# Products in bursts of two key tiles, one 128-column transpose for the row maxima, stacks loaded three groups ahead

## The chip, the cores and the metric

The kernel runs on one core of one Trainium2 chip. The time is that of one execution on the device in microseconds, given as the median of several runs. A core has five engines that run side by side, each with its own list of instructions: TensorE (PE; PEld are its weight loads), VectorE (DVE), ScalarE (ACT), GpSimd (POOL) and SyncE (SP), which here only issues DMA transfers. They wait for each other on semaphores: an instruction waits until a counter has reached a value, and everything behind it on the same engine waits with it.

## What is computed

Four blocks run one after the other on 4 batches of 512 tokens of width 256: a cross attention with a mask (xa0), a self attention (sa0) and a mixture of eight experts (me0), a second cross attention (xa1) and a second mixture (me1). The change touches the three attentions. Each has 16 heads of width 16:

```python
q = split_heads(query @ Wq.T + bq)
k = split_heads(key @ Wk.T + bk)
v = split_heads(value @ Wv.T + bv)
scores = jnp.einsum('bhqd,bhkd->bhqk', q, k) / np.sqrt(HEAD_DIM).astype(np.float32)
attn = jax.nn.softmax(scores, axis=-1)
ctx = jnp.einsum('bhqk,bhkd->bhqd', attn, v)
```

In xa0 the scores are masked before the softmax. Everything is in 32-bit floats; the output of a block is added to its input.

## The kernel before

**Stages.** An attention has a projection stage and an attending stage. The projection goes through the four batches. It makes q and k, splits each value into three 16-bit parts, and stores the parts in DRAM (`q_parts`, `k_parts`, line L700, SP). The attending stage goes through 16 groups, four per batch (`g` is the group in its batch, `G` its number in the stage). A group is four heads of one batch. Its stacks, `qst[g]` and `kst[g]`, are loaded back from DRAM (`load_stacks`, L334): 96 rows, six products of parts times 16 head columns, for each head and token. There is one pair of stack buffers for each of the four `g`.

**Units.** A group has 16 units, `u` = 0 to 15. A unit is one tile of 128 x 512 scores for one head. It is made twice:

- by `scores` (L958), query rows on the partitions, for the row maxima. VectorE reduces each tile to its maximum (`maximum`: L373 with the mask, L377 without). This side runs ahead by 28 units (`LEAD`), so at unit `u` of group g it works on group g + 1 or g + 2.
- by `transposed_scores` (L971), key rows on the partitions, with three further rows that carry minus the row maximum in three 16-bit parts (99 rows). In xa0 a second matmul (L975) adds the mask. ScalarE takes the exponential of each tile (L885) into `probs`.

Both sides rotate over three PSUM banks (`DEEP` = 3), so a tile can be made when the one three units earlier has been read. At a border between batches the rotation starts anew (`before`): the first tile of a batch waits for the last one of the batch before.

**Row maxima.** When the 16 maxima tiles of a group are reduced, `split` on VectorE (L1125 to L1131) writes the three parts into `mparts`. At `u` = 8 TensorE transposes them (`maxima`, L993, four transposes of 12 columns, one for each tile of 128 queries), ScalarE copies the result into `mT`, 12 rows of 512 (L898), and SP moves it into rows 96 to 98 of the next group's `qst` (`shift`, L792). The next group's first `transposed_scores` waits for that.

**Products.** `products` (L985) multiplies the exponentials with the values: for one tile of 128 keys, four matmuls, one for each head, each in its own 32 columns of the array, so the four run side by side. In 32-bit floats each is two instructions in the trace, so a burst is eight. The four key tiles of a group come after units 5, 9 and 13 and, the last one, after unit 1 of the next group. ScalarE then copies the sums (L891), TensorE turns them at `u` = 12 (`turn`, L1016), and VectorE divides by the row sums after unit 13 (`normalise`, L1139 to L1144). In later batches TensorE also turns the output of the batch before (`turn_out`, L1025, in g 1) and projects it (`project_out`, L1036, in g 2 and 3), and VectorE adds it after unit 5 of g 2 and 3 (`residual`, L1165 in xa1, L1171 in sa0, there with `block_input`, L1153 and L1157).

**Order.** Nothing is scheduled by a program: each engine's list is written out by hand in the loops over `g` and `u`. SP's is, for each group: wait until the group two before has been used up and load the stacks of g + 2, wait for `mT` and issue the shift of g + 1, then a piece of the weights of a later stage. The first two groups' stacks are loaded inside the projection stage, between the stores of the second and the third batch.

Of the kernel before, what the change touches and what calls it, by code (L numbers as in the profile page):

```python
# [35 lines left out]
P = 128  # L36
# [4 lines left out]
HG = 4  # L41
# [30 lines left out]
class Memory:  # L72


    def __init__(self, nc, ctx):
# [24 lines left out]
        self.mres = sb("mres", [P, T, HG])  # L100
        self.mparts = sb("mparts", [P, T, PARTS, HG], BF16)
        self.mT = sb("mT", [PARTS * HG, S], BF16)
        self.den = sb("den", [P, T, HG])
# [116 lines left out]
class Attention:  # L220


    def __init__(self, nc, stage, mem, dram, name, w, cross, norms, affine, cols, rows, masked, self_block,
# [40 lines left out]
        self.stacks = [sig(f"stacks{s}", 32) for s in range(NG)]  # L264
        self.shift = [sig(f"shift{s}", 16) for s in range(NG)]
        self.s_ps = sig("s_ps", UNITS)
# [411 lines left out]
def project_sync(sp, a):  # L678
# [34 lines left out]
    def rest_of_batches():  # L713
        context(1)
        if a.fresh:
            sp.wait_ge(a.setup, 13)
            for s in range(NG):
                sp.dma_start(mem.kst[s][ROWS:KROWS, :, :].rearrange("r h (i n) -> r (h i) n", n=P),
                             mem.ones[0:PARTS, :].unsqueeze(1).to_broadcast([PARTS, HG * S // P, P]))\
                  .then_inc(a.shift_ones.sem, 16)  # L720
        if a.masked:
            load_mask(sp, a, 0)
        for b in range(0, B - 2):
            body(b, b + 2)
        for n in range(QK):
            sp.wait_ge(a.stored[n].sem, a.stored[n].at(1))
        load_stacks(sp, a, 0, 0)
        load_stacks(sp, a, 0, 1)
        body(B - 2, None)
        body(B - 1, None)  # L730
# [24 lines left out]
LAST_TURN, LAST_OUT = (5, 2), (3, 4)  # L755
LATE = 2

M_STEP, TURN_STEP = 8, 12
# [25 lines left out]
def attend_sync(sp, a, meanwhile, then=None):  # L784
# [3 lines left out]
    def shift(b, g):  # L788

        G = NG * b + g  # L790
        sp.wait_ge(a.m_sb.sem, a.m_sb.at(G, 1))
        sp.dma_start(mem.qst[g][ROWS:KROWS, :, :], mem.mT[:, :]).then_inc(a.shift[g].sem, 16)  # L792

    def body(b, first, last):
        for g in range(NG):
            G = NG * b + g
            ahead = (b, g + 2) if g < 2 else (b + 1, g - 2)
            if not (last and g >= 2):
                if first and g == 2:
                    for n in range(QK):  # L800
                        sp.wait_ge(a.stored[n].sem, a.stored[n].at(B))
                if not (first and g < 2):
                    sp.wait_ge(a.st_ps.sem, a.st_ps.at(G - 1))
                load_stacks(sp, a, *ahead)
# [71 lines left out]
def attend_scalar(act, a, meanwhile):  # L876
# [16 lines left out]
    def maxima(G, used=None):  # L893
        act.wait_ge(a.m_ps.sem, a.m_ps.at(G, 1))
        if used is not None:
            b, g = used
            act.wait_ge(a.shift[g].sem, a.shift[g].at(b, 16))
        act.activation(mem.mT[:, :], ps[0:PARTS * HG, MISC, 0:S // 2].bitcast(BF16), ACT.Copy)\  # L898
           .then_inc(a.m_sb.sem, 1)
# [43 lines left out]
def attend_tensor(pe, a, meanwhile):  # L943
# [17 lines left out]
    def transposed_scores(b, g, u, first):  # L961
# [4 lines left out]
        if u == 0:  # L966
            pe.wait_ge(a.shift[g].sem, a.shift[g].at(b, 16))
            if a.masked and g == 0:
# [9 lines left out]

    def products(G, g, kt):
        pe.wait_ge(a.p_exp.sem, a.p_exp.at(G, HG * (kt + 1)))  # L980
        if kt == 0:
            pe.wait_ge(a.vg_ready.sem, a.vg_ready.at(G, 1))
            pe.wait_ge(a.ot_sb.sem, a.ot_sb.at(G))
        for h in range(HG):
            ins = pe.matmul(ps[h * VW:(h + 1) * VW, OB, :], mem.vg[g % 2][:, kt, h, :], mem.probs[:, kt, h, :],  # L985
                            start=(kt == 0), stop=(kt == T - 1))
        ins.then_inc(a.pv.sem, 1)

    def maxima(G):
        pe.wait_ge(a.cut.sem, a.cut.at(G, CUTS))  # L990
        take_misc()
        for t in range(T):
            ins = pe.transpose(ps[0:PARTS * HG, MISC, t * P // 2:(t + 1) * P // 2].bitcast(BF16),  # L993
                               mem.mparts[:, t, :, :].rearrange("p a h -> p (a h)"), mem.identb[:, :])
        ins.then_inc(a.m_ps.sem, 1)
        misc[0] = (a.m_sb.sem, a.m_sb.at(G, 1))
# [45 lines left out]
    def body(b, first, last):  # L1042
# [4 lines left out]
        for g in range(NG):  # L1047
            G = NG * b + g
            for u in range(UNITS):
# [8 lines left out]

                at = u - HG - LATE + 1
                if at < 0 and u == LATE - 1 and not (first and g == 0):  # L1060
                    products(G - 1, (g - 1) % NG, T - 1)
                if at >= 0 and at % HG == 0:
                    products(G, g, at // HG)
                if g == 1 and not first and u in OUT_TURNS:
# [37 lines left out]
    G = B * NG - 1  # L1102
    products(G, NG - 1, T - 1)
    turn(G)
# [8 lines left out]
def attend_vector(dve, a, meanwhile, beside=None):  # L1113
# [4 lines left out]
    def split(G):  # L1118
# [4 lines left out]
        m = mem.m[:, :, :]  # L1123
        hi, mid, lo = (mem.mparts[:, :, i, :] for i in range(PARTS))
        dve.tensor_scalar(hi, m, -1.0, None, ALU.mult).then_inc(a.cut.sem, 1)  # L1125
# [709 lines left out]
def program(nc, x, ctxT, mask, wa, wb, wc, cols, rows, b1c, b2, gate0, w1, w2, gate1, we, be, out):  # L1835
# [10 lines left out]
    with ExitStack() as ctx:  # L1846
# [26 lines left out]
        def constants(pool):  # L1873
# [3 lines left out]
            pool.memset(mem.ones[:, :], 1.0).then_inc(setup, 1)  # L1877
            pool.memset(mem.tri[:, :], 1.0).then_inc(setup, 1)
            pool.memset(mem.onehot[:, NT, :], 0.0).then_inc(setup, 1)
            pool.iota(mem.count_i[:, :], [[1, P]], base=0, channel_multiplier=0).then_inc(setup, 1)  # L1880
            pool.iota(mem.number_i[:, :], [[1, 1]], base=0, channel_multiplier=1).then_inc(setup, 1)
            pool.wait_ge(setup, 8)
            for eye in (mem.ident, mem.identb):
# [48 lines left out]
        with nc.Block() as block:  # L1932
# [83 lines left out]
            def _(pe):  # L2016
                pe.wait_ge(setup, 13)
                begin, rest = project_tensor(pe, xa0)
# [72 lines left out]
```

## Time and profile before

| | us |
|---|---|
| median of 3 runs | 1280.65 |
| lowest and highest | 1279.75, 1281.99 |
| the profiled execution | 1274.43 |
| its span, from first to last instruction | 1272.7 |

| engine | busy, us | share |
|---|---|---|
| TensorE matmuls | 1131.4 | 89% |
| VectorE | 838.6 | 66% |
| ScalarE | 660.4 | 52% |
| GpSimd | 210.9 | 17% |

The profiled execution is one more run beside the three. Busy time is the time in which an engine has an instruction in work; matmuls overlap in TensorE's pipeline, so what one costs is read from the distance between starts, not from its duration. The attending stages lie at about 63 to 300 us (xa0), 407 to 630 us (sa0) and 937 to 1162 us (xa1). In the timelines a row is one instruction or several alike behind each other (xN), with start and length; in brackets stands how long the engine was idle before it and what it then waited for.

### The profile page before, as it was taken

How to read it: one execution, taken by the hardware profiler on the slowest of the kernel's cores; microseconds unless marked ns; L12 is line 12 of the kernel's file. 1: busy time of each engine (PE TensorE's matmuls, PEld its weight loads, DVE VectorE, ACT ScalarE, POOL GpSimd, SP SyncE). 2: the span in 40 equal slices, each digit the busy share in tenths (PEclk: the TensorE clock that was granted, in tenths of full speed). 3: DMA queues.
4: the chain of work that ended last, by engine and by line, in shares of the span. 5: the costliest groups of instructions: out<-in, count | busy, mean ns of one | idle time of the engine just before them, and what ended most of it. 6: DMA issues, size and time to landing. Idle time of an engine off the chain costs nothing. (4 is left out here: it accounts for less than half of the span.)

```text
span 1272.7 us, 17810 instructions
## 1 busy us (share of the span) xinstructions
PE 1131.4 (89%) x5693; PEld 544.0 (43%) x5722; DVE 838.6 (66%) x2112; ACT 660.4 (52%) x1341; POOL 210.9 (17%) x272
## 2 busy tenths in 40 slices
PE   7889999999997999999967999996989999998390
PEld 4423343434453223343364666664523333335370
DVE  5878777777478888888762222223888888876722
ACT  3346666666533677677722333332537767674250
POOL 4310000000143000000202222211520010102154
PEclk9989999999999899999967999998989999999795
DMA  8953321221048433543291140103873323211064
GB/s 265 309 169 93 79 57 28 81 52 26 2 154 291 103 91 90 132 97 93 72 375 33 31 161 28 27 13 102 263 241 91 90 59 89 60 37 57 25 171 144
DMA packets 100706, 139.40 MB, mean 110 GB/s; under 512 B 8452, under 2 KB 82632, under 8 KB 99208
## 3 DMA queue, kind: packets, MB, share of 16 engines
q1 hardware_dynamic: 96536, 128.03, 33.6%
q0 software_dynamic: 4080, 10.23, 2.9%
q8 instruction: 48, 0.79, 0.3%
q14 instruction: 42, 0.34, 0.1%
HBM read 86.30 MB, written 52.17 MB: 109 GB/s over the span
## 5 line engine op out<-in xcount | busy, mean ns | idle before, releaser
L885 ACT ACTIVATE r<-ps 128x512 f32<-128x512 f32 x768 | 427.4, 600 | 211.9 <-PE ps L971 122.1
L377 DVE TENSOR_REDUCE m<-ps 128x1 f32<-128x512 f32 x512 | 320.9, 682 | 45.2 <-PE ps L958 44.9
L971 PE MATMUL ps<-r 99*128 99x512 bf16 x768 | 294.3, 388 | 5.6 <-ACT r L885 5.6
L958 PE MATMUL ps<-r 96*128 96x512 bf16 x720 | 280.9, 393 | 20.5 <-DVE m L377 7.0
L373 DVE CUSTOM_DVE_ANT_0 r<-ps,r 128x512 bf16<-128x512 f32 x256 | 170.2, 690 | 60.2 <-PE ps L958 59.6
L985 PE MATMUL ps<-r 128*32 128x512 f32 x1536 | 204.9, 605 | 4.9 <-ACT r L885 3.3
L971 PEld LDWEIGHTS ps<-r 99*128 99x128 bf16 x768 | 74.4, 98 | 211.7 <-ACT r L885 157.3
L958 PEld LDWEIGHTS ps<-r 96*128 96x128 bf16 x720 | 71.3, 99 | 105.9 <-DVE m L377 24.3
L861 POOL COPY r<-r 128x256 f32<-128x256 f32 x48 | 19.0, 399 | 542.1 <-PE ps L985 542.1
L1660 DVE COPY r<-ps 128x512 f32<-128x512 f32 x46 | 31.8, 691 | 91.9 <-PE ps L1707 91.9
L1707 PE MATMUL ps<-r 128*128 x184 | 87.8, 621 | 2.7 <-issue 0.4
L1619 ACT ACTIVATE r<-ps,cols 128x128 f32<-128x128 f32 x46 | 18.5, 453 | 137.8 <-PE ps L1698 137.8
L657 PE MATMUL ps<-r,w 128*128 128x512 f32 x192 | 88.2, 596 | 0.5 <-issue 0.5
L975 PE MATMUL ps<-r,identb 128*128 128x512 bf16 x227 | 87.5, 386 | 0.0
L1732 PE MATMUL ps<-r 128*128 x368 | 83.3, 380 | 1.1 <-ACT r L1629 1.1
L1671 DVE TENSOR_TENSOR r<-ps,r 128x256 f32<-128x256 f32 x46 | 19.5, 425 | 97.0 <-PE ps L1732 68.8
L1732 PEld LDWEIGHTS ps<-r 128*128 128x128 f32 x368 | 69.9, 190 | 20.1 <-issue 11.9
L589 ACT ACTIVATE r<-ps,cols 128x512 bf16<-128x512 f32 x48 | 32.9, 686 | 86.9 <-PE ps L657 72.7
L985 PEld LDWEIGHTS ps<-r 128*32 128x32 f32 x1536 | 30.3, 108 | 84.0 <-ACT r L885 65.3
L537 POOL TENSOR_TENSOR r<-r 128x512 bf16<-128x512 f32 x48 | 55.0, 1164 | 65.5 <-ACT r L594 65.5
L644 PE MATMUL ps<-w,r 128*128 128x256 f32 x192 | 45.5, 392 | 13.6 <-DMA w<-in_wa 7.4
L1629 ACT ACTIVATE r<-ps,b1c 128x128 f32<-128x128 f32 x184 | 49.9, 382 | 12.9 <-PE ps L1715 12.8
(151 smaller groups left out, 1220.5 us busy)
## 6 DMA issues: line engine op xcount, KB each, us to landing
r<-q_parts SPq DMA_DIRECT2D x48, 384.0 KB, 5.2
r<-k_parts SPq DMA_DIRECT2D x48, 384.0 KB, 6.0
k_parts<-r SPq DMA_DIRECT2D x24, 384.0 KB, 3.3
q_parts<-r SPq DMA_DIRECT2D x24, 384.0 KB, 3.1
r<-in_w SPq DMA_DIRECT2D x16, 512.0 KB, 4.9
r<-in_w SPq DMA_DIRECT2D x8, 1024.0 KB, 14.4
k_parts<-r SPq DMA_DIRECT2D x24, 256.0 KB, 3.3
q_parts<-r SPq DMA_DIRECT2D x24, 256.0 KB, 3.1
```

The costliest lines, as they stand in the source:

```text
L373: ins = dve.tensor_tensor_reduce(mem.junk[bank], mem.ps[:, bank, :], mem.mbS[:, t, :], 1.0, FLOOR, ALU.add, ALU.max, out)
L377: ins = dve.tensor_reduce(out, mem.ps[:, bank, :], AX.X, ALU.max)
L537: pool.tensor_tensor(mem.parts[n][:, 2, :], mem.res[n % 2], mem.parts[n][:, 1, :], ALU.subtract).then_inc(a.lo.sem, 1)
L657: ins = pe.matmul(ps[:, QK_BANK + n, :], a.w[:, 0 if of_query(n) else 1, c, (n % C) * P:(n % C + 1) * P], src[:, c, :], start=(c == 0), st ...
L885: act.activation(mem.probs[:, u // HG, u % HG, :], ps[:, ST + (UNITS * g + u) % DEEP, :], ACT.Exp, scale=SCALE).then_inc(a.p_exp.sem, 1)
L958: pe.matmul(ps[:, led_bank(n), :], mem.qst[g][0:ROWS, h, t * P:(t + 1) * P], mem.kst[g][0:ROWS, h, :], start=True, stop=True).then_inc(a.s ...
L971: ins = pe.matmul(out, mem.kst[g][0:KROWS, h, kt * P:(kt + 1) * P], mem.qst[g][0:KROWS, h, :], start=True, stop=not a.masked)
L975: ins = pe.matmul(out, mem.identb[:, :], mem.mbT[:, batch, kt, :].rearrange("p b n -> p (b n)"), start=False, stop=True)
L985: ins = pe.matmul(ps[h * VW:(h + 1) * VW, OB, :], mem.vg[g % 2][:, kt, h, :], mem.probs[:, kt, h, :], start=(kt == 0), stop=(kt == T - 1))
L1629: ins = act.activation(mem.midT[:, f, :], ps[:, TM[f // 4], (f % 4) * P:(f % 4 + 1) * P], ACT.Relu, bias=mem.b1c[:, bass.ds(e * FT + f, 1)])
L1707: ins = pe.matmul(ps[:, UP[k], :], mem.xT[j % 2][:, c, :], w, start=(c == 0), stop=(c == C - 1))
L1732: ins = pe.matmul(ps[:, DOWN[j % 2], 0:D], mem.midT[:, f, :], w, start=(f == 0), stop=(f == FT - 1))
```

## The change

Three things are altered.

1. **Products.** `TOGETHER` = 2: two key tiles are multiplied in one burst of 16 instructions. The first burst comes after unit 9, the second after unit 1 of the next group. Each waits for the exponentials of both its tiles.
2. **Row maxima.** `mparts` becomes one tile of 128 x 128 (48 columns used, the rest zero, set once by GpSimd), and one transpose of 128 columns takes the place of the four. `mT` has 48 rows of 128. The shift becomes four transfers of 3 x 4 x 128 in place of one of 3 x 4 x 512.
3. **Stacks.** `AHEAD` = 3: a group's stacks are loaded when the group three before starts, as soon as the group that used the same buffers has been used up. Three pairs are loaded inside the projection stage.

```diff
--- before.py
+++ after.py
@@ -98,8 +98,8 @@
         self.mres = sb("mres", [P, T, HG])
-        self.mparts = sb("mparts", [P, T, PARTS, HG], BF16)
-        self.mT = sb("mT", [PARTS * HG, S], BF16)
+        self.mparts = sb("mparts", [P, P], BF16)
+        self.mT = sb("mT", [PARTS * T * HG, P], BF16)
         self.den = sb("den", [P, T, HG])
@@ -262,7 +262,7 @@
         self.stacks = [sig(f"stacks{s}", 32) for s in range(NG)]
-        self.shift = [sig(f"shift{s}", 16) for s in range(NG)]
+        self.shift = [sig(f"shift{s}", 16 * T) for s in range(NG)]
         self.s_ps = sig("s_ps", UNITS)
@@ -724,8 +724,8 @@
             sp.wait_ge(a.stored[n].sem, a.stored[n].at(1))
-        load_stacks(sp, a, 0, 0)
-        load_stacks(sp, a, 0, 1)
+        for g in range(AHEAD):
+            load_stacks(sp, a, 0, g)
         body(B - 2, None)
@@ -754,6 +754,8 @@
 LATE = 2
+AHEAD = 3
+TOGETHER = 2
 
@@ -789,18 +791,20 @@
         sp.wait_ge(a.m_sb.sem, a.m_sb.at(G, 1))
-        sp.dma_start(mem.qst[g][ROWS:KROWS, :, :], mem.mT[:, :]).then_inc(a.shift[g].sem, 16)
+        for t in range(T):
+            sp.dma_start(mem.qst[g][ROWS:KROWS, :, t * P:(t + 1) * P],
+                         mem.mT[t * PARTS * HG:(t + 1) * PARTS * HG, :]).then_inc(a.shift[g].sem, 16)
 
     def body(b, first, last):
         for g in range(NG):
             G = NG * b + g
-            ahead = (b, g + 2) if g < 2 else (b + 1, g - 2)
-            if not (last and g >= 2):
-                if first and g == 2:
+            ahead = (b, g + AHEAD) if g + AHEAD < NG else (b + 1, g + AHEAD - NG)
+            if not (last and g + AHEAD >= NG):
+                if first and g + AHEAD == NG:
                     for n in range(QK):
                         sp.wait_ge(a.stored[n].sem, a.stored[n].at(B))
-                if not (first and g < 2):
-                    sp.wait_ge(a.st_ps.sem, a.st_ps.at(G - 1))
+                if G + AHEAD >= NG:
+                    sp.wait_ge(a.st_ps.sem, a.st_ps.at(G + AHEAD - NG + 1))
                 load_stacks(sp, a, *ahead)
@@ -894,8 +898,8 @@
             b, g = used
-            act.wait_ge(a.shift[g].sem, a.shift[g].at(b, 16))
-        act.activation(mem.mT[:, :], ps[0:PARTS * HG, MISC, 0:S // 2].bitcast(BF16), ACT.Copy)\
+            act.wait_ge(a.shift[g].sem, a.shift[g].at(b, 16 * T))
+        act.activation(mem.mT[:, :], ps[0:PARTS * T * HG, MISC, 0:P // 2].bitcast(BF16), ACT.Copy)\
            .then_inc(a.m_sb.sem, 1)
@@ -964,7 +968,7 @@
         if u == 0:
-            pe.wait_ge(a.shift[g].sem, a.shift[g].at(b, 16))
+            pe.wait_ge(a.shift[g].sem, a.shift[g].at(b, 16 * T))
             if a.masked and g == 0:
@@ -976,23 +980,21 @@
 
-    def products(G, g, kt):
-        pe.wait_ge(a.p_exp.sem, a.p_exp.at(G, HG * (kt + 1)))
-        if kt == 0:
+    def products(G, g, first):
+        pe.wait_ge(a.p_exp.sem, a.p_exp.at(G, HG * (first + TOGETHER)))
+        if first == 0:
             pe.wait_ge(a.vg_ready.sem, a.vg_ready.at(G, 1))
             pe.wait_ge(a.ot_sb.sem, a.ot_sb.at(G))
-        for h in range(HG):
-            ins = pe.matmul(ps[h * VW:(h + 1) * VW, OB, :], mem.vg[g % 2][:, kt, h, :], mem.probs[:, kt, h, :],
-                            start=(kt == 0), stop=(kt == T - 1))
-        ins.then_inc(a.pv.sem, 1)
+        for kt in range(first, first + TOGETHER):
+            for h in range(HG):
+                ins = pe.matmul(ps[h * VW:(h + 1) * VW, OB, :], mem.vg[g % 2][:, kt, h, :], mem.probs[:, kt, h, :],
+                                start=(kt == 0), stop=(kt == T - 1))
+            ins.then_inc(a.pv.sem, 1)
 
     def maxima(G):
         pe.wait_ge(a.cut.sem, a.cut.at(G, CUTS))
         take_misc()
-        for t in range(T):
-            ins = pe.transpose(ps[0:PARTS * HG, MISC, t * P // 2:(t + 1) * P // 2].bitcast(BF16),
-                               mem.mparts[:, t, :, :].rearrange("p a h -> p (a h)"), mem.identb[:, :])
-        ins.then_inc(a.m_ps.sem, 1)
+        pe.transpose(ps[:, MISC, 0:P // 2].bitcast(BF16), mem.mparts[:, :], mem.identb[:, :]).then_inc(a.m_ps.sem, 1)
         misc[0] = (a.m_sb.sem, a.m_sb.at(G, 1))
@@ -1056,11 +1058,11 @@
 
-                at = u - HG - LATE + 1
-                if at < 0 and u == LATE - 1 and not (first and g == 0):
-                    products(G - 1, (g - 1) % NG, T - 1)
-                if at >= 0 and at % HG == 0:
-                    products(G, g, at // HG)
+                at = u + 1 - LATE
+                if at == 0 and not (first and g == 0):
+                    products(G - 1, (g - 1) % NG, T - TOGETHER)
+                if at > 0 and at % (TOGETHER * HG) == 0:
+                    products(G, g, at // HG - TOGETHER)
                 if g == 1 and not first and u in OUT_TURNS:
@@ -1100,7 +1102,7 @@
     G = B * NG - 1
-    products(G, NG - 1, T - 1)
+    products(G, NG - 1, T - TOGETHER)
     turn(G)
@@ -1121,7 +1123,8 @@
         m = mem.m[:, :, :]
-        hi, mid, lo = (mem.mparts[:, :, i, :] for i in range(PARTS))
+        mparts = mem.mparts[:, 0:T * PARTS * HG].rearrange("p (t a h) -> p t a h", t=T, a=PARTS)
+        hi, mid, lo = (mparts[:, :, i, :] for i in range(PARTS))
         dve.tensor_scalar(hi, m, -1.0, None, ALU.mult).then_inc(a.cut.sem, 1)
@@ -1876,10 +1879,11 @@
             pool.memset(mem.tri[:, :], 1.0).then_inc(setup, 1)
+            pool.memset(mem.mparts[:, :], 0.0).then_inc(setup, 1)
             pool.memset(mem.onehot[:, NT, :], 0.0).then_inc(setup, 1)
             pool.iota(mem.count_i[:, :], [[1, P]], base=0, channel_multiplier=0).then_inc(setup, 1)
             pool.iota(mem.number_i[:, :], [[1, 1]], base=0, channel_multiplier=1).then_inc(setup, 1)
-            pool.wait_ge(setup, 8)
+            pool.wait_ge(setup, 9)
             for eye in (mem.ident, mem.identb):
```

In two more places a count of the setup semaphore goes from 13 to 14.

TensorE in a group of sa0 before, from the transposes at `u` = 8: L971 and L958 are the two matmuls of a unit, L985 the products.

```order
L993 MATMUL ps<-identb,mparts 12x128 x4
L971 MATMUL ps<-r 128x512
L958 MATMUL ps<-r 128x512
L985 MATMUL ps<-r 32x512 x4
L971 MATMUL ps<-r 128x512
L958 MATMUL ps<-r 128x512
```

The same place in the changed kernel: the lines are now L997, L975, L962 and L990.

```order
L997 MATMUL ps<-identb,mparts 128x128
L975 MATMUL ps<-r 128x512
L962 MATMUL ps<-r 128x512
L990 MATMUL ps<-r 32x512 x8
L975 MATMUL ps<-r 128x512
L962 MATMUL ps<-r 128x512
```

The four transposes have become one, and the second key tile's products stand directly behind the first's. The next place for products before, after unit 13, with the turn of the sums (L1016) ahead:

```order
L1016 MATMUL ps<-ident,r 128x128 x4
L971 MATMUL ps<-r 128x512
L958 MATMUL ps<-r 128x512
L985 MATMUL ps<-r 32x512 x4
```

And in the changed kernel:

```order
L1018 MATMUL ps<-ident,r 128x128 x4
L975 MATMUL ps<-r 128x512
L962 MATMUL ps<-r 128x512
L975 MATMUL ps<-r 128x512
```

Nothing stands between the units from there to unit 1 of the next group.

SP in xa0's projection stage before, where the first stacks (L334) stand between the stores of the second batch and those of the third (L700):

```order
L700 DMA q_parts<-r 128x512
L334 DMA r<-q_parts 96x4x512
L334 DMA r<-k_parts 96x4x512
L334 DMA r<-q_parts 96x4x512
L334 DMA r<-k_parts 96x4x512
L700 DMA k_parts<-r 128x3x512
```

In the changed kernel:

```order
L334 DMA r<-q_parts 96x4x512
L334 DMA r<-k_parts 96x4x512
L334 DMA r<-q_parts 96x4x512
L334 DMA r<-k_parts 96x4x512
L334 DMA r<-q_parts 96x4x512
L334 DMA r<-k_parts 96x4x512
L700 DMA k_parts<-r 128x3x512
```

The third pair has moved ahead of the stores of the last two batches.

## Rows read from the trace of the kernel before

**Rows 1.** Busy time by stretch: us, then each engine's, clock, DMA, GB/s.

```profile
200.00:300.00 100.00, 98.44 (x561) 38.67 (x569) 74.16 (x234) 63.50 (x111) 2.40 (x6) 1.00 0.23 59
...
400.00:500.00 100.00, 92.53 (x480) 29.76 (x479) 87.95 (x169) 64.06 (x122) 7.65 (x12) 0.93 0.46 120
...
1000.00:1100.00 100.00, 99.14 (x576) 37.37 (x580) 85.86 (x175) 71.53 (x137) 6.54 (x10) 1.00 0.27 70
```

**Rows 2.** Timeline of TensorE, a group of xa1: start, length, what [idle before].

```profile
1087.87 0.38 PE L958 MATMUL ps<-r 96*128 96x512 bf16 x1
1088.18 0.39 PE L993 MATMUL ps<-identb,mparts 128*12 128x128 bf16 x4
1088.50 0.39 PE L971 MATMUL ps<-r 99*128 99x512 bf16 x1
1088.72 0.38 PE L958 MATMUL ps<-r 96*128 96x512 bf16 x1
1089.04 1.06 PE L985 MATMUL ps<-r 128*32 128x512 f32 x8
1090.03 0.39 PE L971 MATMUL ps<-r 99*128 99x512 bf16 x1
```

**Rows 3.** Timeline of VectorE in xa1.

```profile
1065.94 0.16 DVE L1139 TENSOR_SCALAR den<-ps 128x16 f32<-128x16 f32 x1
...
1066.82 2.48 DVE L377 TENSOR_REDUCE m<-ps 128x1 f32<-128x512 f32 x4
1069.67 1.29 DVE L377 TENSOR_REDUCE m<-ps 128x1 f32<-128x512 f32 x2 [0.36 <-PE ps L958]
...
1071.71 1.28 DVE L377 TENSOR_REDUCE m<-ps 128x1 f32<-128x512 f32 x2
...
1086.48 0.68 DVE L1165 TENSOR_TENSOR x<-ps,x 128x512 f32<-128x512 f32 x1
```

**Rows 4.** Timelines of VectorE and TensorE in sa0, behind a residual.

```profile
517.26 0.73 DVE L1153 TENSOR_SCALAR w<-x,mv_in,rstd_in 128x256 f32<-128x256 f32 x2
...
519.36 2.47 DVE L377 TENSOR_REDUCE m<-ps 128x1 f32<-128x512 f32 x4
...
520.13 0.38 PE L958 MATMUL ps<-r 96*128 96x512 bf16 x1
...
521.66 0.38 PE L958 MATMUL ps<-r 96*128 96x512 bf16 x1
...
522.08 2.48 DVE L377 TENSOR_REDUCE m<-ps 128x1 f32<-128x512 f32 x4 [0.26 <-PE ps L958]
```

**Rows 5.** Timeline of ScalarE: first and fifteenth copy L898, sa0 and xa1.

```profile
425.79 0.57 ACT L898 ACTIVATE mT<-ps 12x512 bf16<-12x512 bf16 x1
...
616.28 0.57 ACT L898 ACTIVATE mT<-ps 12x512 bf16<-12x512 bf16 x1
...
955.95 0.57 ACT L898 ACTIVATE mT<-ps 12x512 bf16<-12x512 bf16 x1
...
1142.67 0.57 ACT L898 ACTIVATE mT<-ps 12x512 bf16<-12x512 bf16 x1
```

**Rows 6.** Timeline of VectorE in xa0: one batch's mask for the maxima.

```profile
50.42 1.80 DVE L389 TENSOR_SCALAR r<-r 128x512 bf16<-128x512 int32 x4
```

**Rows 7.** Timeline of TensorE in xa0: the first wait for a stack.

```profile
97.53 0.39 PE L958 MATMUL ps<-r 96*128 96x512 bf16 x1 [0.77 <-DMA r<-k_parts]
```

**Rows 8.** DMA issues from 38 to 56 us: size, median us to landing.

```profile
r<-q_parts SPq DMA_DIRECT2D x2, 384.0 KB, 6.8
```

**Rows 9.** Timeline of ScalarE in xa0's projection stage.

```profile
53.37 0.69 ACT L589 ACTIVATE r<-ps,cols 128x512 bf16<-128x512 f32 x1 [4.83 <-DMA k_parts<-r]
```

**Rows 10.** Timeline of SP in xa1: one issue of the shift.

```profile
956.54 0.74 SPq L792 DMA_DIRECT2D r<-mT  x1
```

**Rows 11.** DMA issues of the whole span: a small load, us to landing.

```profile
b1c<-in_b1c SPq DMA_DIRECT2D x1, 32.0 KB, 1.8
```

**Rows 12.** Timeline of ScalarE in xa1's last group.

```profile
1155.18 2.07 ACT L885 ACTIVATE r<-ps 128x512 f32<-128x512 f32 x4 [0.50 <-PE ps L971]
```

More of the change, by code:

```diff
@@ L715, in rest_of_batches @@
         if a.fresh:
-            sp.wait_ge(a.setup, 13)
+            sp.wait_ge(a.setup, 14)
             for s in range(NG):
@@ L2016, in _ @@
             def _(pe):
-                pe.wait_ge(setup, 13)
+                pe.wait_ge(setup, 14)
                 begin, rest = project_tensor(pe, xa0)
```

## The prediction

> **What bounds the kernel now.** I read the busy time by stretches first. In the masked attention (xa0) TensorE is busy 98% of a stretch and VectorE 74%; in the last attention (xa1) it is 99% and 86%, both at the full 2.4 GHz [rows 1]. Then the timelines of one group. An unmasked unit is two 512-column matmuls, L971 for the exponentials and L958 for the maxima. Such matmuls start 0.22 us apart [rows 2], so a unit takes TensorE 0.44; a masked unit has L975 as a third, 0.66. Sixteen units, four bursts of products and the transposes fill TensorE's time: TensorE sets the pace of a group. VectorE has little to spare in the unmasked stages: in xa1 it idles 0.36 us behind a burst before the next tile of scores arrives [rows 3]. Between the two engines lie three banks of scores, and that is what the change has to be tested against.
>
> **What a group costs VectorE.** Maxima come 0.60 apart (four take 2.48, one alone 0.68). The split (L1125 to L1131) stretches one of these steps to 1.44, so it adds 0.84; the quotient (L1139 to L1144) adds 0.88, from 1065.94 to 1066.82 [rows 3]. That is 16 x 0.603 + 0.84 + 0.88 = 11.37 us per group. In groups 2 and 3 of a later batch a residual comes on top: 0.68 less the overlap, 0.63, in xa1, and in sa0 with the block input 2.0 (from 517.26 to 519.36, less the overlap) [rows 3, 4].
>
> **The transpose.** From L958 to the four L993 it is 0.31, and these take 0.32 to the next L971 [rows 2]: 0.63, where L958 alone would take 0.22. So they cost 0.41. One 128-column transpose in the shape of its neighbours is a quarter of 0.22, 0.06, with no change of shape. The bounds are 0.06 and, if the change of shape still costs its 0.09 on either side, 0.24. I take 0.06, for L958 and L971 differ in rows and still follow each other at 0.22. Gain: 0.35 of TensorE's time per group. The copy of it by ScalarE gets a quarter of the columns; ScalarE waits for TensorE anyway, so nothing.
>
> **The products.** From L958 to L985 it is 0.31, that is 0.09 more than L958 needs, and from L985 to the next L971 it is 0.99 [rows 2]. The eight instructions are two passes of four at a time. One instruction lasts 0.60 and the burst 1.06, so the second pass starts 0.46 behind the first, and the last takes 0.53 with its drain. Two key tiles are four passes: 3 x 0.46 + 0.53 = 1.91 in place of 0.99 + 0.99 + 0.09. Gain: 0.16 per merged pair, two pairs per group. The bounds are 1.71, if four passes ran at the 0.43 that 512 columns at half rate take (twice 0.22) and all of the drain were hidden, and 1.98, if nothing is saved. No row shows two key tiles back to back; I take 1.91, built from the one burst that there is.
>
> The Trainium skill, "TensorE: Matmul & The Clock Gate", section "The mechanism", says that a weight load overlaps matmuls in flight only when its row group differs. All these products use the same rows; by that rule every pass would wait for the end of the one before, 4 x 0.60 or more, and the sum would grow by some 45 us. The trace speaks against it: eight such matmuls of 0.60 are through in 0.99.
>
> **What the longer burst does to VectorE** decides the sum. While TensorE is in a burst it makes no scores, and VectorE lives on the three banks. A tile of scores reaches VectorE 0.42 after its L958 starts (521.66, then 522.08). Sa0 shows the case of full banks, just behind a residual: L958 of the tenth unit starts at 520.13, as soon as the maximum begun at 519.36 is done; a burst follows; VectorE, with four maxima in hand from 519.36, is dry at 521.8, and its next begins at 522.08, idle 0.26 [rows 4]. That is the least idle that a burst of 0.99 can leave. With 1.91 it is 0.26 + 0.92 = 1.18, and a group lasts at least 11.37 + 2 x 1.18 = **13.7** us, halves of some 6.85. TensorE would need only 16 x 0.44 + 2 x 2.00 + 0.06 + 0.44 = 11.5; its turns of the output lie in its own waits now. VectorE becomes the bound in the unmasked stages, and the 0.35 + 0.32 saved on TensorE are worth nothing there.
>
> **The sum of the unmasked stages.** Between the copies L898 of the first and of the fifteenth group lie 14 intervals: 186.7 us in xa1, 190.5 in sa0 [rows 5]. After: 12.8 for the first (no quotient in it), 12 x 13.72, 13.6 for the last (VectorE has maxima for a quarter of it only); three borders between batches, where the rotation of the banks makes TensorE wait for VectorE's very last maximum, +1.04 each; four residuals, 2.5 in all or 8.0. That is 196.7 and 202.2: **+10.0** and **+11.7**. The first group's early burst goes away, worth 0.5 in each: **-1**.
>
> **The masked stage.** A unit takes TensorE 0.66 against VectorE's 0.60, half a group 1.91 + 0.09 + 8 x 0.66 + 0.06 = 7.3 against VectorE's 7.0, so TensorE stays the bound and keeps the gain: 16 x 0.35 and 31 merged pairs x 0.16, -10.6. In the first batch VectorE makes the mask of the next one between maxima, four pieces in 1.80 [rows 6], three of them inside one half: 8.4 instead of 7.3, +1.1. The stall for the stack below is 0.77. Together **-10**.
>
> **Stacks three ahead.** Seven times the first L958 of a group waited for its stack, 0.77 us the first and longest time [rows 7], 3.2 in all. These go; six lie in the unmasked intervals and are counted there. But at a stage's start the third pair of loads now stands ahead of the stores of the last two batches. There the queue is full: a load of 384 KB takes 6.8 us to land, and ScalarE waited 4.83 for the stores of k_parts, with VectorE behind it [rows 8, 9]. Another 768 KB at some 300 GB/s are 2.5 us, and two issues about 1. I take 2.0 in xa0, 1.5 in xa1 and 0.5 in sa0, where ScalarE did not wait for these stores: **+4** (0 to 7).
>
> **The shift in four pieces.** One issue takes 0.74 on SP [rows 10], some 0.78 with its gap, so the fourth starts 2.3 later. Behind the transpose come copy and hand-over (0.9), these 2.3 and a landing; small loads land in 1.8 [rows 11]: 5.0. TensorE asks for the shift 5.5 behind the transpose in an unmasked group, 7 in a masked one, and VectorE's pace gives 0.9 more. Nothing, then; with a landing of 4 it would be +1 per unmasked group. The skill's "DMA: Bandwidth & Descriptors", section "Specifications", wants at least 512 B in a piece; these have 256 B where they had 1 KB. No row here has that form, and the sum takes nothing from it.
>
> **The ends of the stages.** There ScalarE is the bound and idles 0.5 per burst [rows 12]; a double burst makes 1.4 of twice 0.5, +0.4, three times less what the output's turns hid. The last burst has two tiles behind the last exponential, +0.92. Together 1.8, three stages: **+5.4**. POOL's one more memset is done before the first weights have landed.
>
> **The sum:** 10.0 + 11.7 - 1 - 10 + 4 + 5.4 = +20 on the profiled 1274.4, so 1294.4. That run stands 6.2 below the median of 1280.65. The forecast for the median is 1280.65 + 20, **1300**.
>
> **Rivals.** A: TensorE stays the bound, since VectorE catches up in the longer stretch between bursts. For it speaks the 99% of xa1, against it the 0.26 of sa0. It would give 48 x 0.67 = -32, -3 for the stacks and +4: 1249. It decides at the length of the burst: at 1.71 an unmasked group takes 13.3, today's mean of 186.7 / 14, and the gain of xa0 decides. Chance 0.10, the faster side.
> B: the passes close up to 1.71. 87 double bursts x 0.20 = -17 against my sum, 1283. For it: 512 columns need no more. Against: the 0.46 seen. Chance 0.08, a quarter faster, half the same.
> C: the four pieces land late, and TensorE waits at each group's first L971: 30 x 1, some 1330. Chance 0.07.
> D: TensorE, now with gaps, is granted 1.2 GHz for stretches, as between 400 and 500 us, where the mean is 0.93 and TensorE busy less [rows 1]. 1320 or more. Chance 0.03.
> Mine has 0.72. This kernel's measurement can tell about 0.2%, 2.6 us. Faster 0.13, same 0.06, slower 0.81. Each 0.1 of burst is worth 9 us and the start of the stages 4: 1280 to 1316 holds mine and B, and leaves out A, C and D.
>
> **What would show it.** L990 x8 with 1.9 to the next L975; VectorE idle for 1.2 behind each burst of sa0 and xa1, and the copies L902 there 13.7 apart; TensorE waiting for VectorE's maxima between bursts; in xa0 groups 0.7 shorter; no L962 that waits for k_parts. It is wrong if groups in xa1 come at 12.6, or if L975 waits for a shift.

## The result and the profile after

The changed kernel takes 1308.83 us in the median of 4 runs (1307.77 to 1309.94), the kernel before 1280.20 (1277.08 to 1281.99, 4 runs). The ratio is 1.0229 (95% interval 1.0211 to 1.0247): 28.6 us slower. The forecast was 1300, 20 us slower. One of the twelve runs of the kernel with late stacks below took 3090 us for no known reason; it moves their median by 0.15 us.

Busy time by stretch in the changed kernel (the columns are those of [rows 1]):

```profile
200.00:300.00 100.00, 98.03 (x577) 41.55 (x576) 75.25 (x246) 64.69 (x119) 2.40 (x6) 1.00 0.19 51
...
1000.00:1100.00 100.00, 90.25 (x512) 34.34 (x512) 79.30 (x163) 63.08 (x127) 5.28 (x9) 0.98 0.27 71
```

In the masked xa0 TensorE is as busy as before. In xa1 it has fallen from 99% to 90% and VectorE from 86% to 79% [rows 1]: both now wait, for each other. The timelines of TensorE and VectorE in the changed kernel, a plain group of xa1, show how:

```profile
1001.82 0.39 PE L975 MATMUL ps<-r 99*128 99x512 bf16 x1
1002.04 0.38 PE L962 MATMUL ps<-r 96*128 96x512 bf16 x1
...
1005.32 0.38 PE L975 MATMUL ps<-r 99*128 99x512 bf16 x1
1006.43 0.39 PE L962 MATMUL ps<-r 96*128 96x512 bf16 x1 [0.73 <-DVE m L377]
1006.75 1.92 PE L990 MATMUL ps<-r 128*32 128x512 f32 x16
1008.60 0.39 PE L975 MATMUL ps<-r 99*128 99x512 bf16 x1
1008.83 0.38 PE L962 MATMUL ps<-r 96*128 96x512 bf16 x1
```

```profile
1002.46 2.48 DVE L377 TENSOR_REDUCE m<-ps 128x1 f32<-128x512 f32 x4 [1.09 <-PE ps L962]
...
1005.69 2.47 DVE L377 TENSOR_REDUCE m<-ps 128x1 f32<-128x512 f32 x4
1009.25 1.29 DVE L377 TENSOR_REDUCE m<-ps 128x1 f32<-128x512 f32 x2 [1.08 <-PE ps L962]
```

The burst of sixteen lasts 1.85 us to the next L975 (1006.75 to 1008.60). VectorE's four maxima from 1005.69 are used up at 1008.16, the next tile reaches it at 1009.25: 1.08 of idle behind each burst, where sa0's fullest banks left 0.26 before [rows 4]. Then TensorE, which needs less time for a unit, catches up until all banks are full and waits itself, here 0.73 at 1006.43. Each waits for the other once per burst, and neither can make it up.

The copies of the row maxima by ScalarE (L902; L898 before), the first and the fifteenth group of sa0 and of xa1, answer [rows 5]:

```profile
421.18 0.26 ACT L902 ACTIVATE mT<-ps 48x128 bf16<-48x128 bf16 x1
...
629.16 0.27 ACT L902 ACTIVATE mT<-ps 48x128 bf16<-48x128 bf16 x1
...
973.50 0.26 ACT L902 ACTIVATE mT<-ps 48x128 bf16<-48x128 bf16 x1
...
1172.24 0.27 ACT L902 ACTIVATE mT<-ps 48x128 bf16<-48x128 bf16 x1
```

From such copies the two profiled executions can be cut into stretches. The first two columns are their lengths in us, the last one the terms of the prediction.

| stretch | before | after | difference | predicted |
|---|---|---|---|---|
| start to the first copy of xa0 | 69.1 | 73.7 | +4.6 | +2 |
| first group of xa0 | 16.6 | 14.8 | -1.8 | in the next |
| 14 intervals of xa0 | 236.0 | 227.0 | -9.0 | -10 |
| to the first copy of sa0 | 90.6 | 93.0 | +2.4 | +2.3 |
| first group of sa0 | 13.5 | 12.7 | -0.8 | -0.5 |
| 14 intervals of sa0 | 190.5 | 208.0 | +17.5 | +11.7 |
| to the first copy of xa1 | 327.2 | 331.1 | +3.9 | +3.3 |
| first group of xa1 | 12.5 | 13.3 | +0.7 | -0.5 |
| 14 intervals of xa1 | 186.7 | 198.7 | +12.0 | +10.0 |
| to the end | 130.0 | 136.0 | +5.9 | +1.8 |
| sum | 1272.7 | 1308.2 | +35.5 | +20 |

The last stretch misleads. The change itself adds 1.15 us to it: the last mixture's first matmul (L1418 before, L1421 after) starts 19.24 and 20.39 us behind the fifteenth group's copy, and some 40 us on the routing's matmuls (L1533 from 1202.00, L1536 from 1232.73) still 59.33 and 60.49. The other 4.8 us arise in the experts behind it, and not by the change: one and the same kernel below (the one transpose with late stacks) takes 135.6 us for the whole stretch in one trace (1260.0 - 1124.4) and 130.0 in another, on another chip (1253.2 - 1123.2). Of the thirteen traces of this document four take 130.0 to 131.3, that of the kernel before among them, and nine 134.2 to 136.1. Without these 4.8 the difference of the two traces is 31, and the medians say 28.6.

### The profile page after: what moved, and what is told of

Same layout as the page of the kernel before. It is cut to its first block and busy times, and to the rows that moved or that the text cites. A ratio compares the mean times of both kernels' runs of the same rounds, so it can differ in the third digit from the quotient of the medians.

```text
span 1308.2 us, 17696 instructions
## 1 busy us (share of the span) xinstructions
PE 1124.9 (86%) x5578; PEld 556.4 (43%) x5578; DVE 829.8 (63%) x2112; ACT 640.0 (49%) x1341; POOL 211.5 (16%) x273
## 5 line engine op out<-in xcount | busy, mean ns | idle before, releaser
L962 PE MATMUL ps<-r 96*128 96x512 bf16 x720 | 285.1, 397 | 43.0 <-DVE m L377 33.3
L975 PE MATMUL ps<-r 99*128 99x512 bf16 x768 | 295.5, 389 | 8.7 <-ACT r L889 5.9
L373 DVE CUSTOM_DVE_ANT_0 r<-ps,r 128x512 bf16<-128x512 f32 x256 | 166.7, 688 | 55.1 <-PE ps L962 54.4
L990 PE MATMUL ps<-r 128*32 128x512 f32 x1536 | 189.6, 612 | 4.4 <-ACT r L889 4.0
L975 PEld LDWEIGHTS ps<-r 99*128 99x128 bf16 x768 | 75.4, 99 | 163.5 <-issue 75.3
L962 PEld LDWEIGHTS ps<-r 96*128 96x128 bf16 x720 | 71.3, 99 | 163.6 <-DVE m L377 83.9
L979 PE MATMUL ps<-r,identb 128*128 128x512 bf16 x256 | 98.4, 384 | 0.0
L657 PE MATMUL ps<-r,w 128*128 128x512 f32 x192 | 92.6, 621 | 0.5 <-issue 0.5
L990 PEld LDWEIGHTS ps<-r 128*32 128x32 f32 x1536 | 40.7, 111 | 92.9 <-issue 67.1
L1575 POOL DMA_INDIRECT r<-token_rows,source x46 | 44.5, 967 | 72.3 <-DVE source L1514 31.8
```

What stands on the lines that cost most here:

```text
L373: ins = dve.tensor_tensor_reduce(mem.junk[bank], mem.ps[:, bank, :], mem.mbS[:, t, :], 1.0, FLOOR, ALU.add, ALU.max, out)
L657: ins = pe.matmul(ps[:, QK_BANK + n, :], a.w[:, 0 if of_query(n) else 1, c, (n % C) * P:(n % C + 1) * P], src[:, c, :], start=(c == 0), st ...
L962: pe.matmul(ps[:, led_bank(n), :], mem.qst[g][0:ROWS, h, t * P:(t + 1) * P], mem.kst[g][0:ROWS, h, :], start=True, stop=True).then_inc(a.s ...
L975: ins = pe.matmul(out, mem.kst[g][0:KROWS, h, kt * P:(kt + 1) * P], mem.qst[g][0:KROWS, h, :], start=True, stop=not a.masked)
L979: ins = pe.matmul(out, mem.identb[:, :], mem.mbT[:, batch, kt, :].rearrange("p b n -> p (b n)"), start=False, stop=True)
```

## Each part alone

Three kernels make one part of the change each, a fourth moves one transfer. All ran on one chip beside the kernel before (1278.39 us there).

**Bursts alone.** The edit to the kernel before is the products' part of the diff, nothing else (here the place of the bursts):

```diff
-                at = u - HG - LATE + 1
-                if at < 0 and u == LATE - 1 and not (first and g == 0):
-                    products(G - 1, (g - 1) % NG, T - 1)
-                if at >= 0 and at % HG == 0:
-                    products(G, g, at // HG)
+                at = u + 1 - LATE
+                if at == 0 and not (first and g == 0):
+                    products(G - 1, (g - 1) % NG, T - TOGETHER)
+                if at > 0 and at % (TOGETHER * HG) == 0:
+                    products(G, g, at // HG - TOGETHER)
```

> Only the products change: two key tiles per burst; transposes, shift and stack loads as in the kernel before. Theory (VectorE runs out of score tiles during the long burst and becomes the bound in the unmasked stages): groups of the unmasked stages 13.6 apart in place of 12.4 to 13.4, the 14 intervals of sa0 and xa1 together some 22 us longer, xa0's groups 0.4 shorter (-6); in all +14 to +24 us against the kernel before, since the shorter transpose and the stacks were worth nothing there anyway. Rival (the loss of the full change comes from the loads at the start of the stages): -5 to -15 us.

Measured: 1309.23 us, ratio 1.0251 (1.0238 to 1.0264), +30.8: the theory's way, and more than its +24. The copies of sa0's and xa1's first and fifteenth group in this kernel, by ScalarE's timeline:

```profile
419.04 0.59 ACT L900 ACTIVATE mT<-ps 12x512 bf16<-12x512 bf16 x1
...
627.03 0.59 ACT L900 ACTIVATE mT<-ps 12x512 bf16<-12x512 bf16 x1
...
968.50 0.59 ACT L900 ACTIVATE mT<-ps 12x512 bf16<-12x512 bf16 x1
...
1168.65 0.57 ACT L900 ACTIVATE mT<-ps 12x512 bf16<-12x512 bf16 x1
```

That is 208.0 and 200.2 us, +17.5 and +13.4, as in the full change, with no stack moved. The rival, that the start of the stages makes the loss, is out. The plain groups are 13.85 apart, 0.26 more than in the full change: the cheap transpose is worth something behind VectorE too, for it delays the last tile ahead of a burst less. VectorE idles 1.34 here behind the burst that has the transposes just ahead of it, and 1.09 behind the other. In xa0 the 14 intervals take 231.2 in place of 236.0.

**The transpose alone.** The transpose, the copy and the shift of the diff, bursts of one and stacks two ahead:

```diff
-AHEAD = 3
-TOGETHER = 2
+AHEAD = 2
+TOGETHER = 1
```

(an edit to the changed kernel).

> Only the row maxima change: one 128-column transpose, a copy of 48 rows by 128, the shift in four pieces. Theory (with bursts of one key tile TensorE is the bound everywhere): 0.35 us less in each group but the last of a stage, -12 to -16 us in all. Rival (four pieces land late, or the transpose hides behind VectorE): 0 or slower.

Measured: 1322.47 us, ratio 1.0351 (1.0336 to 1.0366), **+44**. The rival had the sign, but neither of its causes. Two of the waits of this kernel, for its weight loads (PEld) and its matmuls (us in total, times, longest):

```profile
PEld ps L962 <- DMA r<-k_parts: 56.3, 31, 4.3
...
PE ps L962 <- DMA r<-k_parts: 43.1, 22, 3.9
```

SP's timeline and TensorE's in sa0:

```profile
440.68 2.95 SPq L795 DMA_DIRECT2D r<-mT  x4
443.68 0.42 SPq L1905 DMA_DIRECT2D r<-in_w  x1
444.29 0.32 SPq L334 DMA_DIRECT2D r<-q_parts  x1
444.65 0.48 SPq L334 DMA_DIRECT2D r<-k_parts  x1
...
451.36 0.39 PE L962 MATMUL ps<-r 96*128 96x512 bf16 x1 [2.46 <-DMA r<-k_parts]
```

The shift itself is not late. But its four issues take 2.95 us of SP, and behind them in SP's list stand a weight load and the stacks for the group after next. With two groups of lead the stacks were nearly in time before (eight matmuls waited, 3.4 us in all); 2.2 us later they are not, 22 times and 43.1 us. These waits have a price beyond themselves: between and behind them TensorE is granted 1.2 GHz for some 20 us of sa0's and 10 us of xa1's intervals, which have no such stretch in the kernel before. So the four-piece shift needs the third group of lead, and the full change has it.

**Stacks three ahead, alone.** The lead of three, bursts of one, old transposes, with the third pair inside the projection stage (the edit in part; the loop of SP changes as in the diff of the change):

```diff
-        load_stacks(sp, a, 0, 0)
-        load_stacks(sp, a, 0, 1)
+        for g in range(AHEAD):
+            load_stacks(sp, a, 0, g)
```

> Only the stacks are loaded three groups ahead, the third pair inside the projection stage ahead of the last two batches' stores. Theory: the seven waits for a stack go (-3), the start of the cross attentions waits for the stores of k_parts and q_parts: xa0 and xa1 +4 each; in all +2 to +8 us. Rival (the loads lie beside other work): -3 us.

Measured: 1284.17 us, ratio 1.0045 (1.0032 to 1.0058), +5.8.

**The same with the third pair late.** It is issued behind the first shift, where the kernel before has it:

```diff
     shift(0, 0)
+    for g in range(2, AHEAD):
+        load_stacks(sp, a, 0, g)
     body(0, True, False)
```

> As the stacks alone, but the third pair is issued after the first shift of the attending stage, where the kernel before has it. Theory: the seven waits go and the start of the stages is as before: -2 to -4 us. Rival (the delay at the start does not come from the third pair's place): as the stacks alone, within 1 us.

Measured: 1275.50 us, ratio 0.9972 (0.9961 to 0.9983), -2.9, the forecast value of the waits for the stacks. The place of one pair of loads is worth 8.7 us in three stages. The two traces show where: in the projection of a stage's last batch. There TensorE already makes the first tiles of scores (`early_scores`, L357). From the first of them to the stage's first copy it takes 19.33 us in xa0, 18.57 in sa0 and 18.56 in xa1 with the third pair late, and 22.18, 21.70 and 23.64 with it early: 2.9, 3.1 and 5.1 more. ScalarE's timeline of xa0's projection, with the third pair early and then with it late, beside [rows 9]:

```profile
57.46 0.69 ACT L589 ACTIVATE r<-ps,cols 128x512 bf16<-128x512 f32 x1 [7.92 <-DMA k_parts<-r]
59.48 0.69 ACT L589 ACTIVATE r<-ps,cols 128x512 bf16<-128x512 f32 x1 [1.34 <-DMA k_parts<-r]
```

```profile
55.57 0.69 ACT L589 ACTIVATE r<-ps,cols 128x512 bf16<-128x512 f32 x1 [4.08 <-DMA k_parts<-r]
```

And in sa0 and xa1 with the third pair early. With it late ScalarE waits for no store of k_parts there, nor does it in the kernel before:

```profile
400.92 0.69 ACT L589 ACTIVATE r<-ps,cols 128x512 bf16<-128x512 f32 x1 [6.99 <-DMA k_parts<-r]
...
931.60 0.69 ACT L589 ACTIVATE r<-ps,cols 128x512 bf16<-128x512 f32 x1 [7.92 <-DMA k_parts<-r]
```

In the changed kernel xa0's wait is 8.21 us, with a second of 1.33 behind it. Its DMA issues between 38 and 56 us, size and median us to landing, beside [rows 8]:

```profile
r<-q_parts SPq DMA_DIRECT2D x3, 384.0 KB, 7.5
...
k_parts<-r SPq DMA_DIRECT2D x2, 384.0 KB, 9.2
```

## Is it VectorE?

If VectorE is the bound of the unmasked groups in the changed kernel, less work for VectorE must shorten them, and by more than in the kernel before, where TensorE is the bound. The edit is one line, made to both; the two kernels take the row maxima of the unmasked stages over 256 of the 512 keys, so what they compute there is not the reference's formula:

```diff
-        ins = dve.tensor_reduce(out, mem.ps[:, bank, :], AX.X, ALU.max)
+        ins = dve.tensor_reduce(out, mem.ps[:, bank, 0:256], AX.X, ALU.max)
```

In the changed kernel:

> The changed kernel, but in the two unmasked stages VectorE takes each row maximum over 256 of the 512 columns (its work is cut; the maxima are those of half of the keys). TensorE's list is unchanged. Theory (VectorE, starved during the long bursts, is the bound there): plain groups of sa0 and xa1 fall from 13.6 to 11.3 to 11.6 apart, some -60 us against the changed kernel, about 1250. Rival (the long burst costs TensorE itself, or the shift or ScalarE holds the groups): groups stay at 13 or more, within 10 us of the changed kernel.

Measured: 1263.88 us against the 1308.83 of the changed kernel, taken at another time, -45; ratio to the kernel before 0.9878 (0.9861 to 0.9896). Plain groups are 12.14 apart. In the kernel before:

> The kernel before, with the same cut of VectorE's maxima to 256 columns in the unmasked stages. Theory (there TensorE is the bound): plain groups stay at 12.0 to 12.5, those with a residual and the batch borders get shorter; -10 to -20 us against the kernel before. Rival (VectorE was the bound before too): -60 us as in the changed kernel.

Measured: 1270.06 us, ratio 0.9925 (0.9907 to 0.9944), -9. With the same relief one kernel gains five times what the other does. The theory stands, but its numbers fail: -45 and not some -60, groups of 12.14 and not 11.3 to 11.6, and -9 lies just outside -10 to -20. ScalarE's timeline of the changed kernel with the cut maxima says what is late next:

```profile
970.51 1.58 ACT L889 ACTIVATE r<-ps 128x512 f32<-128x512 f32 x3 [1.34 <-PE ps L975]
972.26 2.56 ACT L889 ACTIVATE r<-ps 128x512 f32<-128x512 f32 x5 [0.17 <-PE ps L975]
976.72 0.60 ACT L889 ACTIVATE r<-ps 128x512 f32<-128x512 f32 x1 [1.91 <-PE ps L975]
```

ScalarE lives on three banks as well. It idles 1.34 and 1.91 behind the bursts, and with its copies fills nearly all the rest of a group: the weight loads of L975 there wait for it (978.35, 978.84 and 979.33, the distance of its exponentials). A long burst starves both readers of the score banks, and VectorE, with 0.60 a tile against ScalarE's 0.48, is only the first to show it.

## The parts that pay

What is left without the bursts: the one transpose with its four-piece shift, and the lead of three with the late third pair. The edit to the changed kernel is `TOGETHER = 1` and the move shown above.

> The one transpose with the shift in four pieces, bursts of one key tile as before, stacks three ahead with the third pair issued after the first shift. Theory (the +44 of the transpose alone came only from the stack loads that stand behind four issues of the shift on SP; three groups ahead they are in time): no wait for k_parts, groups 0.35 shorter than with the late stacks alone, 1275.5 - 14 = 1260 to 1265. Rival (the four pieces themselves hold TensorE): 1280 or more.

Measured: 1257.35 us, ratio 0.9831 (0.9813 to 0.9850), -21.7. That is faster than both kernels, and 2.7 below the range expected. ScalarE's timeline in sa0, two successive copies of a plain interval, first with late stacks alone, then with the transpose too:

```profile
437.49 0.57 ACT L902 ACTIVATE mT<-ps 12x512 bf16<-12x512 bf16 x1
449.94 0.57 ACT L902 ACTIVATE mT<-ps 12x512 bf16<-12x512 bf16 x1
```

```profile
430.58 0.27 ACT L904 ACTIVATE mT<-ps 48x128 bf16<-48x128 bf16 x1
442.67 0.27 ACT L904 ACTIVATE mT<-ps 48x128 bf16<-48x128 bf16 x1
```

12.45 and 12.09: the transpose saves 0.36 us of a group, where the forecast had 0.35. A part of the start is left: in xa1 ScalarE waits 6.1 us for a store of k_parts in this kernel too, and L357 to the first copy takes 20.60 there; why was not looked into. With three groups of lead no matmul waits for a stack, and three weight loads do, 1.2 us in all.

The same with double bursts in the masked stage alone, where TensorE is the bound (the edit in part: `products` and its places take `together(a)` for `TOGETHER`):

```diff
+def together(a):
+    return TOGETHER if a.masked else 1
```

> As the one before, and bursts of two key tiles in the masked stage xa0 alone, where TensorE has 0.66 us of work per unit and VectorE keeps up; one key tile in sa0 and xa1. Theory: another -5 to -7 us, 1254 to 1259. Rival (a burst of two starves VectorE there too): equal or slower than the one before.

Measured: 1257.68 us, ratio 0.9830 (0.9813 to 0.9848): the same as without. In the traces xa0's 14 intervals are 227.0 against 230.2. Both ran once more, beside each other and the kernel before (1272.16 us on that chip):

> The one transpose with late stacks and bursts of one key tile, beside the next kernel on the same chip. Theory and rival: 1256 to 1260 us; it is the base for the next.

> The same with bursts of two key tiles in xa0 alone. Theory (a double burst saves 0.2 us of TensorE and TensorE is the bound in xa0): 4 to 6 us under the kernel before it in this list. Rival (something later in the kernel gives it back, as equal medians of the first comparison say): within 2 us.

Measured: 1254.35 and 1254.48 us, ratios 0.9860 (0.9828 to 0.9892) and 0.9848 (0.9825 to 0.9870). Again no difference. In this pair of traces the copy that opens sa0 is 4.6 us earlier with double bursts (399.74 against 404.37). Sa0's first group gives back 1.6 of it, the way from there to the opening of xa1 2.3 (927.38 against 928.11), and xa1's first group 1.3 (942.93 against 942.33). So xa0's gain is real and was lost outside the stage that made it. In both first groups TensorE is granted 1.2 GHz for a while in all four traces. In this pair the stretch is longer with double bursts: 13.6 us against 10.2 in sa0, 17.1 against 13.6 in xa1. In the first pair the stretches are equally long, 10.2 and 13.6 us, and nothing was given back in these groups, though the medians did not differ either. So the traces put the 1.6 and the 1.3 down to the clock; where the 2.3 went, and why the medians of the first pair are equal, stays open.

Last, the whole change with only the third pair late:

> The whole change, with only the third pair of stack loads moved back behind the first shift. Theory (the start costs what stacks alone against late stacks showed, 8.7 us): 1298 to 1302. Rival (the start of the stages is hidden once the stages are bound by VectorE): 1307 or more.

Measured: 1292.95 us, ratio 1.0162 (1.0137 to 1.0187), +20.8 on that chip. Against the +28.6 of the whole change the start is worth 7.8, close to the 8.7 of the pair above: it is not hidden. The number expected, 1298 to 1302, was for a chip on which the kernel before takes 1280; the ratio gives 1301 there. This difference is between two chips, while that of the pair is within one.

## Why the forecast was right, and where its sizes were off

The sign, the mechanism and the range held. That the total is off by only 9 is partly luck: the clock (6.1 us, below) and the start of the stages (4.7 more) came on top of the forecast, and the ends of the stages, some 2 us less if all three are like xa1's, took part of it back. Step by step:

- **The transpose**: 0.35 forecast, 0.36 measured. Right.
- **The double burst**: 1.91 forecast, 1.85 measured; a merged pair saves 0.22, not 0.16. The bounds of 1.71 and 1.98 held. The Trainium skill, "TensorE: Matmul & The Clock Gate", section "The mechanism", lets a weight load overlap matmuls in flight only when its row group differs. The trace disagrees: sixteen matmuls of 0.6 us each, all on the same rows, are through in 1.85, with weight loads at 1006.75, 1007.20 and 1007.63. The same section also names the background weight buffer, for which loads are pulled ahead; no run here tells whether that is what happens.
- **VectorE's idle**: 1.18 forecast behind each burst, 1.08 measured; plain groups 13.7 against 13.59. The reading that carried the forecast, the 0.26 of idle with full banks [rows 4] plus the longer burst, is good to 0.1 us.
- **Unmasked stages**: +10.0 and +11.7 forecast, +12.0 and +17.5 in the trace. What is missing from the term is mostly what rival D held, given 0.03. Three intervals of the changed kernel stand out: 17.61 and 18.02 in sa0 and 16.18 in xa1, where the same places in another batch take 16.09, 14.83 and 14.80. TensorE's timeline and the stretches (the clock is the third column from the end) in sa0:

```profile
505.82 3.23 PE L990 MATMUL ps<-r 128*32 128x512 f32 x16
508.98 0.39 PE L975 MATMUL ps<-r 99*128 99x512 bf16 x1
...
513.91 1.92 PE L990 MATMUL ps<-r 128*32 128x512 f32 x16
```

```profile
491.00:505.00 14.00, 11.61 (x65) 5.30 (x60) 11.32 (x24) 8.37 (x16) 0.69 (x2) 1.00 0.35 95
505.00:508.50 3.50, 3.42 (x18) 0.70 (x17) 2.02 (x4) 0.81 (x2) 1.58 (x2) 0.51 0.03 7
```

  TensorE was granted 1.2 GHz from 505 to 508.5 us, behind 14 us in which it had been busy 83% (11.61 of 14.00), and a whole double burst fell into it: 3.2 us in place of 1.85. This cost 1.5 + 3.2 + 1.4 = 6.1 us in the three intervals; the kernel before shows no such stretch inside its attending stages once they are under way. Without it the stages are +10.6 and +12.8, a little over the forecast.
- **The masked stage**: -10 forecast, -9.0 in 14 intervals and -1.8 in the first group. Right.
- **The start of the stages**: +4 (0 to 7) forecast, 8.7 measured by the pair of stack kernels. The terms were 2.0 in xa0, 0.5 in sa0 and 1.5 in xa1; from L357 to the first copy the pair has 2.9, 3.1 and 5.1 more, and the changed kernel 2.8, 2.8 and 5.0 more than the kernel before. So xa0's was nearly right and the other two were mis-sized. The 0.5 rested on ScalarE not waiting for these stores in sa0; with the third pair ahead of them it waits, 6.99 us in sa0 and 7.92 in xa1 (stacks alone). In xa0's projection stage of the changed kernel the large stores of k_parts land 9.2 us after their issue, 8.2 in the kernel before.
- **The waits for the stacks**: seven, 3.2 us, in the prediction; the trace of the kernel before has eight, 3.4. They are gone, worth 2.9.
- **The shift**: "nothing" was right for this kernel (its waits for the shift sum to 1.4 us). What the step overlooked is the rest of SP's list behind the four issues: with two groups of lead 44 us. It named the landing of the pieces and not the transfers queued behind them. The Trainium skill's "DMA: Bandwidth & Descriptors", section "Specifications", wants at least 512 B in a piece; with 256 B TensorE's waits for the shift show no cost beyond the 1.4 us.
- **Worth nothing in the unmasked stages**: nearly; the transpose is worth 0.26 us of a group there.
- **The ends of the stages**: +5.4 forecast, 1.8 of it behind xa1's fifteenth group, where 1.15 was measured. All four kernels with double bursts in xa1 have their first mixture matmul 20.4 us behind that copy, the nine others 19.2 to 19.6. The term was too large; which part of it is not known.

So rivals A, B and C are out by the plain groups (13.59, not 12.6), the burst (1.85, not 1.71) and the shift's waits. D was an addition to the forecast case and not a case of its own.

## What to carry to other kernels

Before two bursts on a shared engine are merged to save the switch between them, look at the engines that read its results. What counts is the longest stretch without a new tile against the tiles in the banks: here three tiles of 0.60 us could not bridge 1.85 and the 0.65 from the end of the burst to the next tile (1008.60 to 1009.25). Merges that save TensorE 0.2 us each made a plain group of 12.09, with the one transpose and late stacks, one of 13.59. Where the reader has time to spare, as in the masked stage, the merge is harmless.

A transfer that becomes four costs the queue four issues, and the ones that pay are those behind it. Prefetching further ahead pays for that, but the added first load should not be put in front of stores that somebody waits for: the same load a little later turned +5.8 into -2.9 us.

Parts of a change should be timed apart and together. Alone they cost 30.8, 44.1 and 5.8 us, together 28.6; without the bursts, and with one pair of loads moved, the other two gain 21.7.

## What was not expected of the hardware

- The granted clock of TensorE fell to 1.2 GHz for 3.4 us at a time within the unmasked stages (at 505.1, 583.6, 593.8 and 1020.5 us), behind stretches in which TensorE had waited much; with VectorE's work cut there is no such stretch there, and with the transpose alone, where TensorE waits up to 3.9 us for stacks, there are more. In these traces a slower pace thus brings slower matmuls on top, about 6 us here.
- Four issues of 12 rows by 256 bytes take SP 2.95 us, as much each as one of 12 rows by 1 KB takes (0.74).
- Two profiled executions of one and the same kernel, on two chips, differ by 5.6 us behind the last attention alone (135.6 and 130.0). A difference of two traces is to be held against a third before it is explained.
